# Projections in 64-row pairs, the last bias copied into PSUM by ScalarE, an exponent mask in strided order, and the last tile's rounding on VectorE

## What is computed

```python
x = _layernorm(x + _L0_attn_ref(x, ...))        # 4 narrow blocks (64 channels), then h @ Wout.T + bout
x = _layernorm(x + _L0_xattn_ref(x, ctx, ctx))  # autocorrelation, top 8 shifts, softmax, weighted sum of shifts
x = _layernorm(x + _L0_ffn_ref(x, weight, bias))
# inside _L0_ffn_ref: both operands rounded to 4-bit floats, one power-of-two scale per 32 values
xq = quantize_mxfp4(x)
wq = quantize_mxfp4(weight)
out = jnp.einsum('bsk,nk->bsn', xq, wq) + bias
```

## Time and profile before

| | us |
|---|---|
| median of 3 executions | 324.72 |
| lowest and highest of these | 324.19, 325.27 |
| the profiled execution, its own time | 324.38 |
| its span in the trace | 322.2 |

### The profile page before, as it was taken

One profiled execution on the slowest core, in us unless ns is written; L12 is line 12 of the kernel. 1 busy time (PEld: TensorE's weight loads), 2 busy tenths in 40 slices (PEclk: granted clock), 3 DMA queues, 4 the chain that ended last, 5 costly groups with the idle time before them and its releaser, 6 DMA issues.

```text
span 322.2 us, 4490 instructions
## 1 busy us (share of the span) xinstructions
PE 269.6 (84%) x1088; PEld 110.6 (34%) x1096; DVE 266.8 (83%) x864; ACT 239.5 (74%) x556; POOL 184.4 (57%) x233
## 2 busy tenths in 40 slices
PE   1597788988989887898999999999989899769443
PEld 1223222322323232254543555534544434413110
DVE  5979989889889894458999999999999999876530
ACT  6056789889899798967767789888889785665524
POOL 1027422203204204023399989999999999997792
PEclk9999999999999999999999999999999999996955
DMA  6999999502114002500000000000000010000003
GB/s 208 395 263 341 344 164 219 141 2 63 39 29 132 31 0 40 92 2 1 2 0 1 2 0 2 33 35 35 3 33 34 33 35 34 1 33 35 33 34 130
DMA packets 14415, 24.56 MB, mean 76 GB/s; under 512 B 2611, under 2 KB 3251, under 8 KB 14390
## 3 DMA queue, kind: packets, MB, share of 16 engines
q1 hardware_dynamic: 12310, 20.09, 18.5%
q0 software_dynamic: 2080, 4.19, 7.6%
HBM read 15.89 MB, written 4.19 MB: 62 GB/s over the span
## 4 chain that ended last, share of the span: by engine, by line
POOL 35%; PE 21%; issue 13%; DVE 13%; ACT 13%; DMA 3%; SPq 1%; POOLq 0%; DVEq 0%; ACTq 0%
POOL big L893 5%; POOL big L886 5%; POOL big L899 5%; POOL xq L795 4%; POOL big L877 3%; POOL big L790 3%; POOL X L909 3%; DMA big<-in_xT_dram 3%; ACT L720 2%; PE ps L361 2%; POOL big L892 2%; PE ps L535 2%; PE ps L450 2%; PE ps L476 2%; PE ps L422 2%
## 5 line engine op out<-in xcount | busy, mean ns | idle before, releaser
L1074 DVE SCALAR_TENSOR_TENSOR X<-ps,X 128x512 f32<-128x512 f32 x48 | 31.2, 684 | 15.6 <-PE ps L504 6.6
L621 ACT ACTIVATE big<-X,lnv 128x512 f32<-128x512 f32 x48 | 34.3, 714 | 11.8 <-DVE X L1074 11.7
L372 PE MATMUL ps<-ctx_ring,consts 64*128 64x512 f32 (+1 forms) x96 | 34.9, 633 | 0.0
L422 PEld LDWEIGHTS ps<-consts,big 96*128 96x128 f32 x256 | 30.7, 192 | 6.6 <-DVE big L1109 2.7
L1151 DVE TENSOR_TENSOR big<-ps,ctxf 128x512 f32<-128x512 f32 x48 | 30.4, 681 | 1.9 <-PE ps L458 1.2
L422 PE MATMUL ps<-consts,big 96*128 96x64 f32 x256 | 30.9, 274 | 1.2 <-DVE big L1109 1.1
L649 ACT ACTIVATE X<-X,lnv 128x512 f32<-128x512 f32 x32 | 25.9, 809 | 0.6
L806 POOL TENSOR_TENSOR big<-big 128x512 f32<-128x512 f32 x4 | 5.8, 1443 | 35.4 <-DVE big L1187 25.2
L1139 DVE MATCH_REPLACE8 big<-w,big 128x64 f32<-128x64 f32 x128 | 25.1, 209 | 0.0
L886 POOL TENSOR_TENSOR big<-big 128x512 f32<-128x512 f32 x16 | 20.3, 1267 | 6.5 <-DVE big L1139 6.0
L790 POOL TENSOR_TENSOR big<-X,qs 128x512 f32<-128x512 f32 x20 | 20.9, 1048 | 1.6
(11 more groups left out here) (172 smaller groups left out, 664.5 us busy)
## 6 DMA issues: line engine op xcount, KB each, us to landing
big<-in_xT_dram SPq DMA_DIRECT2D x4, 1024.0 KB, 9.4
ctx_ring<-in_ctx_dram SPq DMA_DIRECT2D x16, 256.0 KB, 4.9
out_dram<-X SPq DMA_DIRECT2D x16, 256.0 KB, 2.0
X<-in_x_dram SPq DMA_DIRECT2D x2, 1536.0 KB, 11.6
X<-rows_sb POOLq DMA_DIRECT2D x1, 3072.0 KB, 21.6
X<-in_wq_dram SPq DMA_DIRECT2D x1, 1024.0 KB, 5.9
X<-in_x_dram SPq DMA_DIRECT2D x2, 512.0 KB, 4.1
X<-rows_sb POOLq DMA_DIRECT2D x1, 1024.0 KB, 8.7
```

The source lines that it names most:

```text
L372: mm(bank(LANE_BANK[lane]), mat((CY_0, CY_1, CY_C)[f])[half, :], ctx_ring[half, r * N:(r + 1) * N], start=True, stop=True).then_inc(s_cfor ...
L422: last = mm(ps[:, 2 * N + j * P + b * L:2 * N + j * P + (b + 1) * L], PQ[0:EVEN, b * N + j * P:b * N + (j + 1) * P], mat(IC_E)[0:EVEN, 0:L ...
L621: squared[k, n] = chain(a(JUNK[k], row(n), ACT.Square, bias=st[:, 0:1], scale=-float(V), accum_out=st[:, 2:3]))
L1074: stt(row(m), bank(b), 0.0, row(m), ALU.add, ALU.add, accum_out=st[:, 0:1]).then_inc(s_sum[k], 1)
```

## The change

1. The output weight stands once on each half of the partitions (`wo`), without zeros. `projection(n)` runs for even n only and issues two 64-row matmuls, one for each half, tile n into bank 0 and tile n + 1 into bank 7; `attended` of both follow each other on VectorE in even steps. Bank 7 is also that of `weight_rest_forms`, so this now waits until the projections that stand there are added, and a projection waits for the product that reads it. In the first part two PSUM banks of the last slot are exchanged, and a wait is added ahead of the first projection.
2. The bias is loaded to all 128 partitions by a second broadcast DMA of 256 KB on SyncE, instead of to three. The memsets of `woz` and `ones` and the split of the bias on VectorE are gone. A new step of ScalarE, `bias_in(n)` at t = n + 8, copies it into bank 1, and `feed_forward(n)` adds to that; it waits for the copy.
3. The exponent mask of each value goes over the row in the order "p (b k) -> p k b": 32 passes over the 16 blocks, a step of 32 values, for both operands.
4. For tile 15 the subtraction of `chosen` and the whole rounding from the scale on run on VectorE (`last_chosen`, `last_quantized`), in H, and not on GpSimd.

```diff
             def projection(n):
-                if here(n):
+                if here(n) and n % 2 == 0:
                     pe.wait_ge(s_hn, 1 if n < PAIRS // 2 else 2)
                     if n == 0:
                         pe.wait_ge(s_wout_in, 32)
                     if n >= 1:
                         pe.wait_ge(s_sum[0], n)
-                    mm(bank(0), H[:, n // 2 * P:(n // 2 + 1) * P], woz[:, n % 2 * V:(n % 2 + 1) * V],
-                       start=True, stop=True).then_inc(s_y, 1)
+                    if n >= 7:
+                        pe.wait_ge(s_pw, 3 * (n - 7) + 1)
+                    for g in range(2):
+                        mm(bank(Y_BANK[g]), H[g * D:(g + 1) * D, n // 2 * P:(n // 2 + 1) * P], wo[g * D:(g + 1) * D, :],
+                           start=True, stop=True).then_inc(s_y, 1)
...
                     if n >= 1:
                         pe.wait_ge(s_pw, 3 * n - 2)
+                    pe.wait_ge(s_sum[0], min((n + 6) // 2 * 2 + 2, PAIRS))
                     mm(bank(7), mat(XW_C), WT, start=True, stop=True).then_inc(s_w, 1)
...
                     if n == 0:
                         pe.wait_ge(s_qe[0], VC)
-                        pe.wait_ge(s_bias, 1)
-                    if n >= 1:
-                        pe.wait_ge(s_sum[2], n)
-                    mm(bank(1), ones[:, :], bias3[:, :], start=True, stop=False)
+                    pe.wait_ge(s_bias, n + 1)
                     pe.wait_ge(s_qe[1], n + 1)
...
+            def bias_in(n):
+
+                if here(n):
+                    if n == 0:
+                        act.wait_ge(s_rows, 32)
+                        act.wait_ge(s_hn, 2)
+                    else:
+                        act.wait_ge(s_sum[2], n)
+                    copy(bank(1), rows_sb[:, V:2 * V]).then_inc(s_bias, 1)
...
             for t in range(PAIRS + 10):
                 squares(0, t)
+                bias_in(t - 8)
                 corr_out(t - 3)
...
-                do(ts(MB.bitcast(I32), VB.bitcast(I32), 0x7F800000, None, ALU.bitwise_and))
+                do(ts(MB.bitcast(I32).rearrange("p (b k) -> p k b", k=BLK), VB.bitcast(I32).rearrange("p (b k) -> p k b", k=BLK),
+                      0x7F800000, None, ALU.bitwise_and))
...
+            def last_chosen(n):
+
+                if n == LAST:
+                    dve.wait_ge(s_mr, n + 1)
+                    dve.wait_ge(s_wt, n)
+                    tt(WN, G, REST, ALU.subtract).then_inc(s_wn, 1)
+
+            def last_quantized(n):
+
+                if n == LAST:
+                    vb, mb = H[:, 0:N], H[:, N:2 * N]
+                    top, inverse = (qs[:, (2 * (n % 2) + k) * NBLK:(2 * (n % 2) + k + 1) * NBLK] for k in range(2))
+                    dve.wait_ge(s_amax[1], n + 1)
+                    do(tt(inverse.bitcast(I32), ends[:, :], top.bitcast(I32), ALU.subtract))
+                    do(tt(blocks(vb), blocks(row(n)), inverse.unsqueeze(2).broadcast_to([P, NBLK, BLK]), ALU.mult))
+                    do(ts(mb.bitcast(I32), vb.bitcast(I32), 0x7F800000, None, ALU.bitwise_and))
+                    ch(ts(mb, mb, 0.25, MAGIC, ALU.max, ALU.mult))
+                    do(ts(vb, vb, 1.5, -1.5, ALU.min, ALU.max))
+                    do(tt(vb, vb, mb, ALU.add))
+                    do(tt(vb, vb, mb, ALU.subtract))
+                    dve.wait_ge(s_qt[1], n)
+                    tt(blocks(xq[:, :]), blocks(vb), top.unsqueeze(2).broadcast_to([P, NBLK, BLK]), ALU.mult
+                       ).then_inc(s_qd[1], 1)
...
             for t in range(PAIRS + 11):
                 fed(t - 10)
-                attended(t)
+                if t % 2 == 0:
+                    attended(t)
+                    attended(t + 1)
                 weight_products(t - 6)
                 block_scales(t - 7)
+                last_quantized(t - 7)
                 without_largest(t - 5)
+                last_chosen(t - 5)
                 largest(t - 4)
```

More of the change, by code:

```diff
@@ L23 @@
 PAIRS = ROWS // P
+LAST = PAIRS - 1
 HC = ROWS // 2
@@ L119 @@
 LANE_BANK = (6, 7, 5, 4)
+Y_BANK = (0, 7)
 def context_lanes():
@@ L177, in build @@
         w2_all = sb("w2_all", [P, DEPTH * 2 * D])
-        woz = sb("woz", [P, 2 * V])
-        ones = sb("ones", [SPLIT, P], BF16)
+        wo = sb("wo", [P, V])
         wqT = sb("wqT", [P, VC * V], BF16)
@@ L210, in build @@
         HB = [bank(b) for b in (4, 2, 0, 5)]
-        HB_LAST = [bank(b) for b in (2, 4, 7, 3)]
+        HB_LAST = [bank(b) for b in (2, 4, 5, 6)]
         XC = [bank(3), bank(1)]
@@ L235, in build @@
         s_dve, s_actc, s_pool = sem("s_dve"), sem("s_actc"), sem("s_pool")
-        (s_zero, s_eps, s_mag, s_tanh, s_winc, s_bc, s_idb, s_winmm, s_b1, s_base, s_b1sum, s_w1s, s_sq1, s_var1, s_rs1, s_xn1, s_silu, s_scan,
+        (s_eps, s_mag, s_tanh, s_winc, s_bc, s_idb, s_winmm, s_b1, s_base, s_b1sum, s_w1s, s_sq1, s_var1, s_rs1, s_xn1, s_silu, s_scan,
          s_xc, s_sq2, s_var2, s_rs2, s_xn2, s_w2c, s_hidmm, s_act, s_mlp, s_hn) = (
-            sem(n) for n in ("s_zero", "s_eps", "s_mag", "s_tanh", "s_winc", "s_bc", "s_idb", "s_winmm", "s_b1",
+            sem(n) for n in ("s_eps", "s_mag", "s_tanh", "s_winc", "s_bc", "s_idb", "s_winmm", "s_b1",
                              "s_base", "s_b1sum", "s_w1s", "s_sq1", "s_var1", "s_rs1", "s_xn1", "s_silu", "s_scan", "s_xc", "s_sq2", "s_var2",
@@ L289, in _ @@
             sp.dma_start(consts[:, IDENT * P:], consts_in[:, IDENT * P:]).then_inc(s_mats, 16)
-            sp.dma_start(rows_sb[0:SPLIT, V:2 * V], rows[V:2 * V].partition_broadcast(SPLIT)).then_inc(s_brow, 16)
             for cc in range(2):
@@ L313, in _ @@
                 sp.dma_start(ctx_ring[:, r * N:(r + 1) * N], pair_rows(ctx_in, r // 2, r % 2)).then_inc(s_ctx[r], 16)
-            sp.wait_ge(s_zero, 1)
             for g in range(2):
-                sp.dma_start(woz[g * D:(g + 1) * D, g * V:(g + 1) * V], woutT).then_inc(s_wout_in, 16)
-            sp.dma_start(rows_sb[:, 0:V], rows[0:V].partition_broadcast(P)).then_inc(s_rows, 16)
+                sp.dma_start(wo[g * D:(g + 1) * D, :], woutT).then_inc(s_wout_in, 16)
+            for k in range(2):
+                sp.dma_start(rows_sb[:, k * V:(k + 1) * V], rows[k * V:(k + 1) * V].partition_broadcast(P)
+                             ).then_inc(s_rows, 16)
             def load_x(k0, k1, s):
@@ L504, in feed_forward @@
                         last = mm(bank(1), xqT[:, c * P:(c + 1) * P], wqT[:, c * V:(c + 1) * V],
-                                  start=False, stop=(c == VC - 1))
+                                  start=False, stop=(c == VC - 1), skip_group_check=True)
                     last.then_inc(s_f, 1)
@@ L550, in slot @@
                 if early:
+                    pe.wait_ge(s_fe[1], LANE_USES[1])
                     projection(0)
@@ L776, in _ @@
             chain = Chain(pool, s_pool)
-            g_.memset(woz[:, :], 0.0).then_inc(s_zero, 1)
-            g_.memset(ones[:, :], 1.0)
             chain.then_wait(g_.memset(ends[:, :].bitcast(F32), 2.0 ** 127))
@@ L841, in _ @@
                     pool.wait_ge(s_x, 32)
-                    pool.wait_ge(s_rows, 16)
+                    pool.wait_ge(s_rows, 32)
                     add_bout(0, WROW, s_xb)
@@ L880, in chosen @@
             def chosen(n):
-                if here(n):
+                if here(n) and n < LAST:
                     pool.wait_ge(s_mr, n + 1)
@@ L1016, in _, with identity_rounded @@
             v_.tensor_copy(base[:, 0:1], bank(2)[:, DEPTH:DEPTH + 1]).then_inc(s_base, 1)
[L1018 to L1035 removed]
+            def identity_rounded():
+                dve.wait_ge(s_mats, 16)
                 v_.tensor_copy(ident_bf[:, :], mat(IDENT)).then_inc(s_idb, 1)
@@ L1082, in attended @@
                         dve.wait_ge(s_ln[0], n - SETS + 1)
-                    residual(0, n, 0)
+                    residual(0, n, Y_BANK[n % 2])
             def crossed(n):
@@ L1192, in slot @@
                 if m == 0:
-                    bias_rows()
+                    identity_rounded()
                 elif first and s == 0:
```

18 lines of the change are left out of this document (removed).

## The result

The changed kernel takes 394.8 us in the median of four executions (389.8 to 396.6), the kernel before 325.0. The ratio of 1.205, with a 95% interval of 1.1945 to 1.2154, is that of the two fast executions (389.8 and 393.3 us, median 391.6), since the two slow ones lie over 1.5% above the fastest. Slower was forecast, but the median of 394.8 us lies 16 us above the upper end of the range (379), and 391.6 lies 13 above it.

The account below looks back on a forecast made before the run. GpSimd was taken to bound the middle of the kernel before, at 9.86 us a round. Forecast: 324.4 + 25.8 (ring) + 15.3 (clock) + 1 (pairs) - 2 (last tile) = 364.5 us, range 346 to 379.

Parts of the forecast that it names:

- The ring of waits: Tile loop: ScalarE waits 2.84 us for feed-forward and correlation matmuls between bias copy and corr_out; rounds 12.5 us, +25.8 us.
- B: ScalarE finds its way and the new wait at L450 sets the round; about 329 us; chance 0.05.
- C: GpSimd stays the bound, ScalarE's room swallows the copy; strided mask leaves the shared port alone; 320.7 us; chance 0.04.
- A: Granted clock stays at 1.00 in the same slow loop; 349.2 us; chance 0.27.
- The clock: Loop gaps over 2.5 us drop TensorE to half rate in six rounds, 2.55 us each: +15.3 us, bounds 0 and 23.
- The pairs: Paired projections share bank 7, so L450 waits and VectorE stands 1.7 us at even tiles; 0 to +3.4, taken +1 us.
- The mask: VectorE's strided mask pass stays 0.42 or becomes about 0.7 us, fitting VectorE's room; nothing on the sum.
- The last tile: Tail: selection on VectorE about -1.6, rounding -3.1, later sum +1.5, serial last tiles; -4 to +0.5, taken -2 us.

Follow-up runs that it names:

- the first experiment: The changed kernel with the bias copy alone undone, the bias coming again from the three-row matmul; 350.9 us, ratio 1.080 to the kernel before.

## Why the prediction was wrong, and where it was right

**The ring of waits: right.** Forecast was 2.84 us of waiting ahead of corr_out, measured 2.86; the round at full clock 12.5 us, and 13.1 with a pair, measured 12.3 and 13.0; eleven of them 133.0, measured 135.4 with fillers, which are 3.4 us over the forecast in the last four rounds and 1.0 under it in the first seven. TensorE's idle time was to be 3.7 us and was 3.63. Rivals B and C are out: corr_out had nothing in hand, and moving the copy to where it has brings the old round back. A, the clock at 1.00, is out by the trace; even with the fillers, which keep the clock up, the kernel takes 359.9 us and not A's 349.2, because A has the pairs at +1 us too.

**The clock: right in kind, the term mis-sized.** It was 6 falls at 2.55 us, 15.3 us. Measured in the traces are 164.9 - 135.4 = 29.5 us; the traced execution is 5 us longer than the 391.6, so in the faster ones it may be some us less. Round by round against the same kernel with fillers (17.4 against 13.0, 12.3 and 12.3, 18.1 and 13.0, 12.1 and 12.3, 17.1 and 13.0, 12.6 and 12.3, 16.5 and 12.3, 15.4 and 12.1, 14.5 and 12.1, 15.7 and 12.1, 13.4 and 10.8) there are eight lengthened rounds, at 3.7 us each. The granted clock was at half for 74.5 of these 164.9 us, in nine stretches of 3.4 to 10.2 us. Three things were missed. The prediction let 1.7 us of a stretch of 6.8 fall into the idle time, where it costs nothing; in the round shown above the stretch of 6.8 us began 1.0 us behind the end of the idle time, and elsewhere at most 1.3 us ahead of it (284.76, for a feed-forward at 286.09), and five of the nine last 10.2 us. The slow stretch does not only strike the feed-forward and correlation matmuls: ScalarE waits again, 1.68 us, for the transposes behind them, which the prediction put at 0.6 in three rounds, at full clock. And all rounds of the second half fall, the short ones too, behind idle times of 2.42 and 2.65 us. The bound of nine falls at 2.55 us, 23 us, had the count right and the price of one too low. By the rule of the Trainium skill's page TensorE: Matmul & The Clock Gate, section "HAM oscillation — how this bites in real kernels", the matmuls start slow behind every wait between bursts; the nine stretches agree with it better than the six that were taken, while the waits of 2.73 us ahead of 211.36 and 241.54, behind which the clock stayed at 1.00, do not.

**The pairs: the term that failed.** +1 us, with 0 to 3.4 as bounds; alone they cost 16.7, of which 10.1 stay at full clock. This term also stands for the +1 us ahead of feed_forward(0), where 19.1 were measured. The wait at L453 was seen, and its size nearly so (1.7 us forecast on VectorE's side; 2.4 to 2.7 on TensorE's, 2.2 us of time a pair). What failed is the step from there: only two of five waits were charged, a shorter TensorE was counted as a gain though GpSimd bounds the loop, and the idle time was not put through the reasoning on the clock that the bias copy had had. The projections were fillers themselves: without them the first query forms come after 3.61 us of idleness, and in the traces of the changed kernel and of the pairs alone the tile loop starts at half clock. Of the +19.1 us 9.3 go when fillers stand there. Taken by parts, the pairs alone show 10.3 (187.75 against 177.50) and the copy alone 3.3 (180.81); 5.5 are left, which no run assigns. Two waits of the changed kernel there, and the windows behind them:

```profile
154.23 1.24 PE L453 MATMUL ps<-big,consts 128*128 128x512 f32 x2 [2.41 <-DVE X L1069]
...
178.19 1.31 PE L453 MATMUL ps<-big,consts 128*128 128x512 f32 x2 [2.63 <-DVE X L1069]
```

```profile
156.00:164.00 8.00, 8.00 (x26) 4.40 (x23) 5.25 (x29) 1.53 (x5) 1.55 (x2) 0.50 0.00 1
180.00:188.00 8.00, 8.00 (x29) 4.73 (x26) 5.90 (x31) 1.82 (x6) 3.89 (x6) 0.50 0.00 0
```

Here the clock was at 0.50 for 8 us, where with the pairs alone, behind a wait of 2.42 us at the same place, it was 1.00 from 172 to 188 us. So waits of nearly one length were followed by a fall in one kernel and not in the other. That may be why executions of the pairs alone spread over 20 us; what decides is not settled. It also leaves open how much of the +19.1 us another execution would show.

**The mask: wrong by its premise.** It was put at nothing because VectorE has room in the slow loop. No run isolates it there; where GpSimd bounds it costs 2.3 us. The prediction priced the mask's own length (0.42 to 0.7, measured 0.61) and not its neighbour's. Rival C had the strided order leave the port alone, which it does not. By the rule of the Trainium skill's page VectorE: DVE Perf Modes, section "Mode 2x_2P", the two-port form asks for nothing of the step; the top difference of 0.67 us beside it agrees in that the contention is there, while that section has nothing on the longer pass of 0.61 us.

**The last tile: right alone, open in the change.** -2 forecast, -2.1 alone. The changed kernel's tail is 4.5 us shorter than before, but so is that of the kernel with the bias copy alone (32.9 us), where the last tile is as before: the short tail comes with the slow loop ahead of it, and what the last tile's part gives in the change is not shown. The last rounding there takes from 376.32 to 381.60, 5.3 us (forecast 4.5, before 7.6), since two passes are longer than was assumed.

**The parts don't add.** Alone they cost +16.7, +68.1, +2.3 and -2.1, together 85.0 us; the change costs 66.6. That in a loop that the ring slows down the pairs' wait and the mask are partly covered would explain it, and the pair rounds with fillers fit (13.0 us against 12.3, 0.7 us where the pairs cost 2.2 without the ring), but no run separates the parts. Nor do the small parts add: pairs, mask and last tile come to 16.9 us alone and to 25.7 in the first experiment.

## What to carry to other kernels

Before a step is put into an in-order engine's list, look at what stands right behind it: if that waits for work that stands behind the new step's consumer on another engine, all of it becomes one chain, and an engine with a quarter of its time free turns into the bound. The same copy a few places earlier cost nothing that could be measured here. And wherever an edit makes TensorE wait longer, or takes matmuls out that bridged a gap, price the clock as a term of its own: half rate for every matmul that others wait for until it is back, not only for the next ones.

## What was not expected of the hardware

Matmuls whose result nobody uses bought 31.7 us in the changed kernel (391.6 to 359.9) and 37.7 us with the copy alone (393.3 to 355.6): TensorE was kept at 2.4 GHz by them from 200 to 280 us. The idle times of 3.2 to 4.0 us ahead of the feed-forward in the loop were each followed or overlapped by 1.2 GHz, in both of these kernels without fillers; the one of 3.61 us at 133.75 with the copy earlier was not. Ones of 2.4 to 2.7 us were followed by it in some places (at 178.19 in the changed kernel) and not in others (at 176.49 with the pairs alone). A pass of VectorE over int32 with a step of 32 values in SBUF took 0.61 us against 0.42, and in the median 1.25 against 1.00 beside GpSimd.
